# Two-layer graph attention kernel: the store of the values leaves the attention block in both layers, the second layer projects keys, values, queries, and the fourth query group is stacked ahead of the bias

## The reference

```
n = src.shape[0]
for l in range(L):                                    # L = 2
    q = ((x @ Wq[l].T + bq[l]) * scaling).reshape(n, H, DH)
    k = (x @ Wk[l].T).reshape(n, H, DH)
    v = (x @ Wv[l].T).reshape(n, H, DH)
    scores = jnp.einsum('ehd,ehd->eh', q[tgt], k[srcidx])     # one score for each of 20000 edges
    m = jax.ops.segment_max(scores, tgt, num_segments=n)
    p = jnp.exp(scores - m[tgt])
    s = jax.ops.segment_sum(p, tgt, num_segments=n)
    w = p / (s[tgt] + 1e-16)
    agg = jax.ops.segment_sum(w[:, :, None] * v[srcidx], tgt, num_segments=n)
    attn = agg.reshape(n, D) @ Wo[l].T + bo[l]
    x = _batchnorm(x + attn, g1[l], beta1[l])
    ff = jax.nn.relu(x @ W1[l].T + b1[l]) @ W2[l].T + b2[l]
    x = _batchnorm(x + ff, g2[l], beta2[l])
return _layernorm(x, ln_g, ln_b)
```

## Time and profile before

| | |
|---|---|
| time before, median of 3 runs | 1133.38 us (1133.23, 1133.38, 1137.29) |
| the profiled execution's own time | 1137.21 us |
| its span, first to last instruction | 1135.4 us |
| TensorE matmul busy | 1040.7 us, 92% |
| VectorE / ScalarE / GpSimd busy | 775.9 / 593.3 / 307.0 us |
| mean granted TensorE clock | 0.969 |
| DMA, mean over the span | 85.10 MB, 75 GB/s |
| first scores of attention, layer 0 and 1 | 252.8 us and 710.9 us |

### The profile page before, as it was taken

The page is one execution under the profiler, slowest core; times in us unless marked ns, Lnnn a source line. Parts: engine busy times, 40 slices in busy tenths (PEclk is TensorE's granted clock), DMA queues, the critical chain, the costliest instruction groups (busy, mean ns, idle before and its releaser), DMA issues. The chain is left out here.

```text
span 1135.4 us, 18973 instructions
## 1 busy us (share of the span) xinstructions
PE 1040.7 (92%) x6636; PEld 865.6 (76%) x6636; DVE 775.9 (68%) x2429; ACT 593.3 (52%) x1108; POOL 307.0 (27%) x306
## 2 busy tenths in 40 slices
PE   4899899989899999999899999889999999989943
PEld 2677677787788888887799897768888888879831
DVE  6667565657577777777488710757777777738788
ACT  5452232346466666666335533656666666632444
POOL 1000000004344444443033100434444444303204
PEclk9899899999899999999999999999999999999976
DMA  6033301458412112113203414751211211322203
GB/s 143 23 129 101 114 23 45 100 145 196 98 38 60 37 39 62 38 39 111 102 1 120 97 40 103 165 136 38 60 38 37 60 37 37 110 85 59 39 1 91
DMA packets 51072, 85.10 MB, mean 75 GB/s; under 512 B 15518, under 2 KB 33818, under 8 KB 50724
## 3 DMA queue, kind: packets, MB, share of 16 engines
q1 hardware_dynamic: 50980, 83.92, 29.8%
HBM read 36.50 MB, written 21.61 MB: 51 GB/s over the span
## 5 line engine op out<-in xcount | busy, mean ns | idle before, releaser
L939 PE MATMUL banks<-k_stack,q_stack 128*125 128x416 f32 (+1 forms) x960 | 299.9, 399 | 10.9 <-DMA q_stack<-q_split 7.3
L1035 DVE CUSTOM_DVE_ANT_0 probs<-banks,scores_bias 125x416 f32<-125x416 f32 (+1 forms) x480 | 267.3, 582 | 60.5 <-PE banks L939 56.1
L919 POOL TENSOR_SCALAR probs<-probs,mass_inv 125x1250 f32<-125x1250 f32 x160 | 210.7, 1317 | 347.7 <-DVE mass_inv L1044 347.7
L953 PE MATMUL banks<-ident,probs 125*125 125x125 f32 x1600 | 260.4, 278 | 7.9 <-DVE probs_t L1026 4.7
L953 PEld LDWEIGHTS banks<-ident,probs 125*125 125x125 f32 x1600 | 242.9, 189 | 31.4 <-issue 22.0
L1005 ACT ACTIVATE probs<-probs,neg_peak 125x1250 f32<-125x1250 f32 x160 | 213.4, 1334 | 53.2 <-DVE neg_peak L1058 53.2
L994 ACT ACTIVATE probs_t<-banks 125x500 f32<-125x500 f32 x320 | 152.3, 477 | 118.9 <-PE banks L953 118.9
L968 PE MATMUL banks<-probs_t,v_pair 125*64 125x250 f32 x1600 | 186.2, 379 | 0.9 <-ACT probs_t L994 0.9
L939 PEld LDWEIGHTS banks<-k_stack,q_stack 128*125 128x125 f32 x960 | 148.0, 192 | 39.4 <-issue 17.0
L968 PEld LDWEIGHTS banks<-probs_t,v_pair 125*64 125x64 f32 x1600 | 107.5, 136 | 54.2 <-ACT probs_t L994 1.3
L1026 DVE COPY probs_t<-banks 125x500 f32<-125x500 f32 x160 | 108.1, 675 | 57.1 <-PE banks L953 57.1
(11 more groups left out here) (251 smaller groups left out, 1434.5 us busy)
## 6 DMA issues: line engine op xcount, KB each, us to landing
q_stack<-q_split SPq DMA_DIRECT2D x160, 125.0 KB, 2.3
scores_bias<-edge_bias SPq DMA_DIRECT2D x8, 1171.9 KB
edge_bias<-bias_row SPq DMA_DIRECT2D x10, 585.9 KB
k_stack<-k_lo SPq DMA_DIRECT2D x16, 312.5 KB, 4.3
resid<-residual SPq DMA_DIRECT2D x2, 2500.0 KB, 9.7
values<-v_stage SPq DMA_DIRECT2D x2, 2400.0 KB
residual<-t SPq DMA_DIRECT2D x4, 625.0 KB, 3.2
xs<-in_x SPq DMA_DIRECT2D x5, 480.0 KB
```

What stands on the lines that cost most here:

```text
L919: nc.gpsimd.tensor_scalar(probs[:, u % 4, :], probs[:, u % 4, :], mass_inv[:, u % 4:u % 4 + 1], 1.0, ALU.mult, ALU.mult).then_inc(att["pro ...
L939: mm = nc.tensor.matmul(pb[0:NT, t % 5, 0:sn], q_stack[:, n % 2, half, part, tile * NT:(tile + 1) * NT], k_stack[:, head * N + s0:head * N ...
L953: mm = nc.tensor.transpose(pb[0:NT, 5 + t % 2, j * NT:(j + 1) * NT], probs[:, u % 4, (j0 + j) * NT:(j0 + j + 1) * NT], ident[0:NT, 0:NT])
L1035: nc.vector.tensor_tensor_reduce(out=probs[:, slot % 4, s0:s0 + sn], in0=pb[0:NT, t % 5, 0:sn], in1=scores_bias[:, (n % GROUPS) * GROUP + ...
```

## The change

There are four edits. The store of the values becomes a function, `values_out`, and is issued before the attention block: in the prologue behind the key copies of pairs 0 and 1, in the second layer behind the first bias rows and all key copies, once the values are copied. The second layer's projections run in the order keys, values, queries, and the weights' places are exchanged with it. The first bias rows of the second layer wait for the first copied value product, where they waited for all query products; GpSimd's first split there waits for the first three query products. In attention the DMAs of the fourth query group (`stacked(sp, 3)`) stand ahead of the bias rows of group 3.

```
-                 dict(wv=place("wv_nat1", [P, DC, D], F32, "R8"), wq=place("wq_nat1", [P, DC, D], F32, "RP", 10240),
+                 dict(wq=place("wq_nat1", [P, DC, D], F32, "R8"), wv=place("wv_nat1", [P, DC, D], F32, "RP", 10240),
...
-                K_JOBS[0:8] + turns("wq") + K_JOBS[8:] + Q_JOBS[0:6] + turns("wv") + Q_JOBS[6:] + V_JOBS)
-        RING_OF = (dict(wq=0, wv=1, wk=0), dict(wk=1, wq=0, wv=2))
+                K_JOBS[0:8] + turns("wv") + K_JOBS[8:] + V_JOBS[0:6] + turns("wq") + V_JOBS[6:] + Q_JOBS)
+        RING_OF = (dict(wq=0, wv=1, wk=0), dict(wk=1, wv=0, wq=2))
...
+        def values_out(sp):
+
+            for rows in SPREAD:
+                sp.dma_start(v_d.rearrange("(t p) d -> p t d", p=NT)[rows, :, :], v_stage[rows, :, :]).then_inc(v_stored, 16)
...
-                for c in range(DC):
+                for c in range(2):
+                    k_stacked(sp, 0, c)
+                values_out(sp)
+                for c in range(2, DC):
                     k_stacked(sp, 0, c)
...
                     stacked(sp, 2)
-                    for rows in SPREAD:
-                        sp.dma_start(v_d.rearrange("(t p) d -> p t d", p=NT)[rows, :, :], v_stage[rows, :, :]).then_inc(v_stored, 16)
                     for k in range(2):
                         sp.wait_ge(k_stored[k], 32 * (DC // 2))
+                    stacked(sp, 3)
                     bias_part(3 * GROUP, 4 * GROUP)
-                    stacked(sp, 3)
                     bias_part(4 * GROUP, 5 * GROUP)
...
                         for c in range(DC):
                             k_stacked(sp, 1, c)
-                        sp.wait_ge(proj["copied"], len(Q_JOBS))
+                        sp.wait_ge(proj["copied"], 1)
                         first_bias(sp)
+                        sp.wait_ge(proj["copied"], len(V_JOBS))
+                        values_out(sp)
                         for n in range(2):
                             stacked(sp, n)
...
-                        pool.wait_ge(proj["copied"], len(Q_JOBS))
+                        pool.wait_ge(proj["copied"], len(V_JOBS) + 3)
```

More of the change, by code:

```diff
@@ L1132, in _ @@
                         sp.wait_ge(oph["h1_lo_last"], 2)
-                        sp.dma_start(w_nat[1]["wq"][:, :, :], weight(gnn["Wq"], DC)[:, DC:2 * DC, :]).then_inc(proj["wq"], 16)
+                        sp.dma_start(w_nat[1]["wv"][:, :, :], weight(gnn["Wv"], DC)[:, DC:2 * DC, :]).then_inc(proj["wv"], 16)
                         for i in range(FC):
                             sp.wait_ge(oph[f"r_lo{i}"], 3)
-                        sp.dma_start(w_nat[1]["wv"][:, :, :], weight(gnn["Wv"], DC)[:, DC:2 * DC, :]).then_inc(proj["wv"], 16)
+                        sp.dma_start(w_nat[1]["wq"][:, :, :], weight(gnn["Wq"], DC)[:, DC:2 * DC, :]).then_inc(proj["wq"], 16)
                         for c in range(DC):
```

## The result

| | |
|---|---|
| changed kernel, median of 7 runs | 1128.24 us (1126.14 to 1131.2) |
| kernel before, median of its 7 runs | 1135.88 us (1129.97 to 1139.08) |
| ratio | 0.9938, 95% interval 0.9919 to 0.9956: 7.0 us faster (5.0 to 9.2) |
| the same comparison on another chip (e5, below) | 0.9920, interval 0.9907 to 0.9933: 9.1 us faster (7.6 to 10.6) |
| the profiled execution's own time | 1131.2 us, span 1129.4 us |

The kernel became faster, as forecast, but 1128.24 lies above the forecast range of 1119.5 to 1127.0.

The account below looks back on a forecast made before the run. TensorE, busy 92% of the span, was held back in attention by late group 3 queries. From 1133.38 us, -12.7 for the stalls and +1.3 at the boundary (-11.4), +1.0 held back, gave 1123.0 us; range 1119.5 to 1127.0.

Parts of the forecast that it names:

- The stall and its removal: Attention, both layers: group 3's queries land late behind store and bias rows; removing this gains 12.7 us.
- the eight slots: Attention slots 8 to 15: 34.4 us in layer 0 and 34.5 in layer 1, to become 28.1 in both.
- the wait, the half clock and ScalarE's wait: Attention: TensorE's wait for queries, slow clock after it, ScalarE's wait for the store; all inside the pace difference, none added.
- The bias rows of group 3 as the next late thing: Attention, slot 12: rival that VectorE waits up to 2.6 us per layer for them, 1128.2 at most; chance 0.11.
- The first layer's boundary: Prologue end, layer 0: SyncE issues the last key pair behind the store, delaying first scores 0 to 1.9 us.
- I take +1.3, nearer the full queue: Layer 0's boundary: the cost chosen for SyncE's held-up issue of key pair 3, from 0 to 1.9 us.
- upper bound of 1.9: Layer 0's boundary: the most that issuing the last key pair into a full queue was to cost, 1.9 us.
- one pair of DMAs issued into a full queue: Profile row used for layer 0's boundary: two DMAs took 3.02 us to issue, behind a 9 to 12 us backlog.
- The level: Whole kernel: the starting time from which the sum was taken, 1133.38 us, the median of the runs.
- I take 1 us of the gain as absent from the median runs: Whole kernel: the profiled execution stood 3.8 us above the median, perhaps from half-clock time, so 1.0 us was added back.
- Nothing of layer 1's queries became late: Answers the slower rival: layer 1's group 1 queries meet the store's backlog, landing near 716, 1130.4 us; chance 0.06.
- this rate would make the boundary free: Layer 0's prologue: at 341 GB/s the store takes 7.5 us, ends at 250.0 and costs the boundary nothing; sum 1.3 lower.

Follow-up runs that it names:

- e5: The changed kernel run again without an edit, on another chip: ratio 0.9920 to the kernel before.
- e2: The changed kernel with the old order in attention, group 3's queries behind its bias rows: ratio 0.9906 to the kernel before.
- e1: The kernel before with only group 3's queries moved ahead of its bias rows, the store staying in attention: ratio 0.9971 to the kernel before.
- e3: The changed kernel with layer 0's store of the values back in attention, layer 1 unchanged: ratio 0.9931 to the kernel before.
- e7: The changed kernel with layer 0's store cut in two, half in the prologue and half in attention: ratio 0.9908 to the kernel before.
- e6: The kernel before run again without an edit: one execution, 1139.16 us.
- e11: The changed kernel with the stored values laid out by partition, same bytes in fewer, longer runs: ratio 0.9928 to the kernel before.
- e4: The changed kernel with layer 0's copies of key pairs 2 and 3 moved from the prologue into attention: ratio 0.9869 to the kernel before.
- e12: The changed kernel with layer 0's key pairs 2 and 3 copied in attention and the stored values laid out by partition: ratio 0.9891 to the kernel before.
- e9: The kernel of e4 run again beside the other versions on one chip: ratio 0.9881 to the kernel before.
- e8: The changed kernel with layer 1's projections in the old order keys, queries, values, its store behind the last projection: ratio 1.0001 to the kernel before.
- e10: The kernel before with layer 0's last key pair issued in attention, ahead of the store: ratio 1.0001 to the kernel before.

## Why the prediction was wrong

**The stall and its removal: right.** The gain was read from the pace of the eight slots, 12.7 us; it measured 12.6. That the wait, the half clock and ScalarE's wait must not be added one by one was right as well. The queries land 2.2 to 2.4 us after issue, as written.

**The bias rows of group 3 as the next late thing: right for this kernel.** No wait appeared, with both orders (changed, e2). With the store still in attention it does appear, 3.0 to 3.5 us (e1, e3).

**The first layer's boundary: the mechanism right, the size wrong.** This is the step that failed: "I take +1.3, nearer the full queue". It measured 3.0 us, and 2.5 in e5, and its upper bound of 1.9 was too low too. The bound came from one pair of DMAs issued into a full queue, 3.02 us, and the 1.3 from scaling it down, "as the backlog is less deep than that row's 9 to 12 us". The backlog was indeed less deep, and no deeper than forecast. When the pair was issued, some 0.5 MB of the store had yet to start by the trace's packets, and pair 2's 0.64 MB, where the forecast had 4 us of the store and pair 2. Yet the issue took 3.88 us, longer than that row's. So a hold-up must not be scaled by the depth of the backlog; e7's pair 2 shows the same. The pair's DMAs are of 320 KB and that row's of 128 KB; whether this is why they are held up longer has not been tried apart.

**The level: wrong by the runs that were at hand.** The sum started from 1133.38, the median of three runs. Seven runs of the kernel before give 1135.88, and 17 on each of three occasions 1136.8 to 1138.0. From 1135.88 the same sum ends at 1125.5, inside the range. The profiled execution's 1137.21 was the ordinary one, and the step "I take 1 us of the gain as absent from the median runs" took it for an exception: e6 has the same two stalls, 34.0 and 34.9 us. It takes both errors to leave the range: the level alone ends at 1125.5, the boundary alone at 1124.7, both together at 1127.2.

**What the sum is with measured terms:** -12.6 + 3.0 = -9.6 us (e5: -10.1). The second comparison, 9.1 (7.6 to 10.6), agrees. The first, 7.0 (5.0 to 9.2), lies just under it. In the two traces themselves the parts leave nothing over (e5, above), but lengths of the prologue in single executions differ by over 5 us. The changed kernel's two medians agree, 1128.24 and 1127.91, and it is the seven runs of the kernel before that lie lower than its later ones; that their spread made the first comparison low is argued and not shown. Of the 5.2 us between 1123.0 and 1128.24, the level is 2.5, the boundary 1.7 and attention 0.1; the 1 us held back went the other way, and 1.9 stay open.

**The rivals.** The order of queries and bias mattered only with the store in place (e1 against e2). Nothing of layer 1's queries became late: the first four were issued into the backlog over 8.79 us from 690.6 (2.39 us with an empty queue), and the second group still landed near 707, some 4 us before the first scores at 711.1. The forecast had said 708. The Trainium skill ("DMA: Bandwidth & Descriptors", section Bandwidth) gives 341 GB/s for a transfer of 1 MB, measured on loads into SBUF that GpSimd issues. That this rate would make the boundary free did not come true: the boundary cost 3.0 us, and this queue gave 213 to 215 GB/s from 242 to 254, when the store was most of what it moved (e5, e11).

## What to carry to other kernels

A large transfer that nobody waits for still has two prices, and they are paid in different places: what queues behind it lands late, and the engine that issues the next DMAs is held up by what is still queued. So a transfer is moved to where the queue's next users are few, and what the issuing engine would do between it and a barrier is put behind the barrier, if nobody needs it earlier (e4). Issuing the store from another engine was not tried. And a stall is priced by the pace around it, not by the named wait: with the named wait taken away alone (e1), the next two transfers held the same place, and of 12.6 us of attention only 2.5 were won.

## What the runs showed of the hardware

SyncE's issue of two 320 KB DMAs took 1.10 us with little queued (before, e6, e7). It took 3.4 to 3.9 us some 12 us behind the issue of a 2.56 MB store, with the store's last 0.25 to 0.5 MB and another such pair still queued (changed, e2, e5, e11). With a seventh of the packets it was still 3.74 us (e11), so it did not follow their number; but the store's own issue fell from 4.28 to 2.52 us with them, and that of four bias DMAs from 4.86 to 2.25 (e12 against e9). It did not follow the bytes ahead either: another pair took 3.35 us behind half of the store (e7) and 2.89 behind all of it (changed). What sets the length of a hold-up stays open.

TensorE's granted clock fell to 0.50, the level of 1.2 GHz, during its wait at the boundary in all five executions where this lasted 5.5 to 6.0 us (changed, e2, e5, e8, e11). Where it lasted 3.0 to 3.3 us, it fell in three executions (before, e1, e3) and held in two (e6, e7). After 1.5 to 1.6 us it held in all four (e4, e9, e10, e12).
